# Sixteen small products on TensorE: spread among 32 large ones, or in one burst behind them

## The chip, the cores and the metric

The kernel runs on one core of a Trainium2 chip. The metric is the device time of one execution, in microseconds; lower is better.

## The reference

Two graph layers over N = 8192 nodes with 128 features, each with a residual and a layer norm. The adjacency matrix is 8192 x 8192, 32-bit integers of 0 and 1.

```python
# layer 0: attention
Wh = h @ W
e = (Wh @ a1)[:, None] + (Wh @ a2)[None, :]
e = where(e > 0, e, 0.2 * e)
e = where(adj > 0, e, -9e15)
x = layernorm(x + elu(softmax(e, axis=1) @ Wh))
# layer 1: mean over the neighbours
x1 = a @ x / sum(a, axis=1)
x = layernorm(x + concat([x1, x]) @ weight + bias)
```

## The kernel before

**The first layer.** The exponential of a leaky ReLU of s_i + t_j is one of two products, depending on the sign of s_i + t_j. So the kernel never computes a score for the matmul: it makes two 0/1 masks for each tile (an edge with a positive score, an edge with a negative one) and multiplies them with two sets of factors. The nodes are taken in 32 groups of 256 rows (two tiles of 128). For a group there are four accumulators (two tiles, positive and negative), `acc`, each a sum over 64 column tiles.

The 64 column tiles of a group are done in 8 steps `h` of 8 tiles. One step, `multiply` (lines 653 to 677), is 4 accumulators x 8 tiles = 32 masked products (line 668): a 128x128 mask of one byte per element as the weights, and 259 columns of factors that stream past it. ScalarE makes the sign masks ("levels", line 465) in a ring of 8 slots, VectorE joins them with the edges (lines 974 and 981) in place, and TensorE waits for `mask_ok` ahead of each step. The last masked product of a step signals `mask_used`, for which ScalarE waits before it fills that slot again for the next group. The last product of each accumulator in step 7 signals VectorE, which scales and adds the accumulators (`add_negative`, lines 1010 to 1020: `acc_done` for the first three, `mask_used` for the fourth) before TensorE may start the next group's sum in the same bank.

**The packing.** The edges come as 32-bit integers and are packed into 16-bit words, one bit an edge, which both layers unpack. 512 rows by 2048 columns are a chunk; four chunks make a block of two groups. GpSimd starts the load of a chunk (`load_adj`, line 360, which narrows it to bytes), VectorE shifts and ors its four row tiles into one byte tile (`join`, lines 913 and 916), and TensorE multiplies the byte tile with powers of two (`pack_tile`, line 615): 16 products, each with 128x128 bytes as the weights and 32 columns of `pack_w` that stream past, into a bank of `pack_ps` that alternates with the chunk. The last of them signals `packed`. ScalarE then copies the words out (`copy_words`, line 421), and GpSimd starts the next load into that chunk's slot.

The first four chunks are packed ahead of or between the first steps, without a join: `pack_bits` (line 627) makes 64 products in one row, 4 for each of the 16 positions. All later chunks are packed inside the steps of groups 1 to 29. The order is written out by hand (lines 698 to 705): the dictionary gives for a pair of steps `c` the chunk that is packed in its second step.

```python
group(1, {1: (1, 0), 2: (1, 1), 3: (1, 2)})
group(2, {1: (1, 3), 2: (2, 0), 3: (2, 1)})
group(3, {1: (2, 2), 3: (2, 3)})
with pe.Fori(2, NR - 1) as n:
    group(PAIR * n, {1: (n + 1, 0), 3: (n + 1, 1)})
    group(PAIR * n + 1, {1: (n + 1, 2), 3: (n + 1, 3)})
```

NR is 16. `packable` (line 608), ahead of such a step, waits until the chunk is joined and the words of the chunk before the last are copied out.

**The second layer** (line 746 above all) starts when the first is done, and works from the packed words.

Of the kernel before, what the change touches and what calls it, by code (L numbers as in the profile page):

```python
# [41 lines left out]
UNIT = 16  # L42
HALF = 8
# [15 lines left out]
def adj_resnorm_kernel(nc, x, adj, w0, a0, w1, b1, consts, out):  # L59
# [21 lines left out]
    with ctx:  # L81
# [494 lines left out]
        def _(pe):  # L576
# [35 lines left out]
            def pack_tile(c, j):  # L612

                nibbles = adj_ring[:, c, 0, j * P:(j + 1) * P].bitcast(F8)
                return pe.matmul(pack_ps[c % 2][:, j * WPR:(j + 1) * WPR], nibbles, pack_w[:, 0, :], start=True, stop=True)  # L615
# [37 lines left out]
            def multiply(g, h, factors_in=False, first=False, pack_chunk=None):  # L653

                pe.wait_ge(mask_ok, 8 * g + h + 1)
                pe.sem_inc(masks_there, 1)
                for a in range(2 * TPG):
                    b, neg = a // 2, a % 2
                    if factors_in and a < 2:
                        pe.wait_ge((e_low_ok, f_low_ok)[neg], min(h // 2, UPG - 1) + h // 7 + 1)  # L660
                    if h == 0 and not first:
                        pe.wait_ge(neg_added if neg else pos_scaled, TPG * (g - 1) + b + 1)
                        pe.sem_inc(sums_read, 1)
                    for j in range(HALF):
                        jj = h * HALF + j
                        mask = level_bytes[:, h % MASK_SLOTS, j, b * P:(b + 1) * P] if neg else \
                            edge_bytes[:, (h // 2) % EDGE_SLOTS, (h % 2) * HALF + j, b * P:(b + 1) * P]
                        m = pe.matmul(acc[a][:, 0:WIDE_ROW], mask, factors[:, neg, jj, 0:WIDE_ROW],  # L668
                                      start=(jj == 0), stop=(jj == NJ - 1))
                        if h == 7 and a < 2 * TPG - 1 and j == HALF - 1:  # L670
                            m.then_inc(acc_done, 1)
                        if a == 2 * TPG - 1 and j == HALF - 1:
                            m.then_inc(mask_used, 1)
                        if pack_chunk is not None and j % 2:
                            w = pack_tile(pack_chunk, (a * HALF + j) // 2)
                if pack_chunk is not None:
                    w.then_inc(packed, 1)

            def group(g, packs):
                for c in range(UPG):  # L680
                    for h in (2 * c, 2 * c + 1):
                        n, pack_chunk = packs.get(c, (0, None)) if h % 2 else (0, None)
                        if pack_chunk is not None:
                            packable(n, pack_chunk)
                        multiply(g, h, pack_chunk=pack_chunk)
# [7 lines left out]
            for c in range(UPG):  # L693
                if c == 1:
                    pack_bits(3)
                for h in (2 * c, 2 * c + 1):
                    multiply(0, h, c == UPG - 1 or h % 2 == 0, True)
# [615 lines left out]
```

## Time and profile before

| | us |
|---|---|
| median of 3 runs | 1489.55 (1487.83 to 1490.34) |
| the profiled execution | 1488.95 |
| its span, first to last instruction | 1487.2 |
| TensorE busy in the span | 1449.8 (97%) |
| VectorE busy | 995.0 (67%) |
| ScalarE busy | 936.7 (63%) |

The span holds three parts: some 50 us until the first masked product, the first layer up to about 1000 us, and the second layer. PE stands for TensorE's matmuls, PEld for its weight loads, DVE for VectorE, ACT for ScalarE, POOL for GpSimd. A matmul's end is modelled and runs past the start of the next one, so the pace of a stream of matmuls is read from start to start.

### The profile page before, as it was taken

How to read it: one execution, taken by the hardware profiler on the slowest of the kernel's cores; microseconds unless marked ns; L12 is line 12 of the kernel's file. 1: busy time of each engine (PE TensorE's matmuls, PEld its weight loads, DVE VectorE, ACT ScalarE, POOL GpSimd, SP SyncE). 2: the span in 40 equal slices, each digit the busy share in tenths (PEclk: the TensorE clock that was granted, in tenths of full speed). 3: DMA queues.
4: the chain of work that ended last, by engine and by line, in shares of the span. 5: the costliest groups of instructions: out<-in, count | busy, mean ns of one | idle time of the engine just before them, and what ended most of it. 6: DMA issues, size and time to landing. Idle time of an engine off the chain costs nothing.

```text
span 1487.2 us, 33752 instructions
## 1 busy us (share of the span) xinstructions
PE 1449.8 (97%) x11982; PEld 1095.5 (74%) x11982; DVE 995.0 (67%) x2835; ACT 936.7 (63%) x2289; POOL 118.2 (8%) x199
## 2 busy tenths in 40 slices
PE   7599999999999999999999999999999999999997
PEld 7478888888888888888888888884454545454543
DVE  4997887888788888878878888773433343334332
ACT  6989999999999999999999999940000000000000
POOL 1001100100010010001001000000000000000000
PEclk9789999999999999999999999999999999999999
DMA  9969997788688868877886882041000000000000
GB/s 172 111 75 103 120 102 91 83 94 95 84 87 96 93 78 95 94 88 84 94 95 83 88 96 37 19 116 49 22 19 17 14 21 15 20 14 21 14 14 14
DMA packets 99182, 101.42 MB, mean 68 GB/s; under 512 B 4416, under 2 KB 66368, under 8 KB 99136
## 3 DMA queue, kind: packets, MB, share of 16 engines
q0 software_dynamic: 33792, 67.11, 45.4%
q1 hardware_dynamic: 65344, 33.70, 8.7%
q8 instruction: 28, 0.46, 0.1%
q14 instruction: 18, 0.15, 0.0%
HBM read 289.48 MB, written 12.65 MB: 203 GB/s over the span
## 4 chain that ended last, share of the span: by engine, by line
PE 92%; DVE 1%; DMA 0%; issue 0%; POOL 0%; ACT 0%; SPq 0%; DVEq 0%; POOLq 0%; ACTq 0%
PE acc L668 60%; PE pack_ps L746 29%; PE pack_ps L615 1%; PE turn_ps L768 1%; PE acc L781 1%; PE turn_ps L757 0%; DMA level_ring<-x_rows 0%; POOL one L380 0%; DMA x_parts<-parts 0%; DVE stats L1078 0%; DVE edge_ring L981 0%; DVE level_ring L1177 0%; DVE adj_space L913 0%; DVE mv L1085 0%; DVE level_ring L1090 0%
## 5 line engine op out<-in xcount | busy, mean ns | idle before, releaser
L465 ACT ACTIVATE level_ring<-s_row,cols 128x256 fp8e4<-128x256 f32 x1984 | 803.7, 495 | 0.0
L668 PE MATMUL acc<-factors,edge_ring 128*128 128x259 f16 x4096 | 549.3, 274 | 8.0 <-DVE edge_ring L981 5.6
L668 PE MATMUL acc<-factors,level_ring 128*128 128x259 f16 x4096 | 548.1, 274 | 0.0
L746 PE MATMUL pack_ps<-adj_space,factors 128*128 128x512 fp8e4 x2048 | 449.9, 379 | 0.8 <-issue 0.8
L668 PEld LDWEIGHTS acc<-factors,edge_ring 128*128 128x128 fp8e4 x4096 | 366.1, 98 | 58.0 <-issue 8.6
L668 PEld LDWEIGHTS acc<-factors,level_ring 128*128 128x128 fp8e4 x4096 | 366.5, 98 | 48.9
L746 PEld LDWEIGHTS pack_ps<-adj_space,factors 128*128 128x128 f16 x2048 | 200.4, 98 | 231.9 <-issue 1.1
L974 DVE TENSOR_TENSOR level_ring<-level_ring,edge_ring 128x1024 uint16<-128x1024 uint16 x256 | 171.1, 689 | 104.3 <-ACT level_ring L465 93.9
L1148 DVE TENSOR_SCALAR adj_space<-words 128x512 uint16 (+1 forms) x448 | 96.2, 287 | 146.8 <-PE pack_ps L746 146.7
L615 PE MATMUL pack_ps<-pack_w,adj_space 128*128 128x32 bf16 x960 | 170.7, 178 | 0.0
L981 DVE TENSOR_TENSOR edge_ring<-edge_ring,level_ring 128x1024 uint16<-128x1024 uint16 x256 | 166.7, 683 | 0.1
L564 ACT ACTIVATE level_ring<-pack_ps 128x256 f32<-128x256 f32 x32 | 10.5, 381 | 226.9 <-PE pack_ps L746 226.9
L556 ACT ACTIVATE level_ring<-turn_ps 128x512 f32<-128x512 f32 x16 | 9.6, 597 | 224.1 <-PE turn_ps L757 224.1
L904 DVE TENSOR_SCALAR edge_ring<-words 128x512 uint16 (+1 forms) x448 | 106.4, 298 | 9.1 <-issue 6.6
L378 POOL TENSOR_SCALAR one<-mv 128x2 f32<-128x2 f32 x64 | 18.7, 292 | 1085.1 <-DVE mv L1085 1085.1
L615 PEld LDWEIGHTS pack_ps<-pack_w,adj_space 128*128 128x128 fp8e4 x960 | 91.6, 95 | 14.1
L1177 DVE SCALAR_TENSOR_TENSOR level_ring<-acc,cols,level_ring 128x128 f32<-128x128 f32 x64 | 19.4, 345 | 92.6 <-PE acc L781 92.6
L913 DVE SCALAR_TENSOR_TENSOR adj_space<-adj_space 128x1024 int32<-128x1024 int32 x60 | 73.1, 1219 | 0.0
L360 POOL DMA_DIRECT2D adj_space<-in_adj x64 | 51.3, 802 | 255.9 <-PE pack_ps L615 199.1
L421 ACT ACTIVATE words<-pack_ps 128x512 f32 (+1 forms) x64 | 38.2, 596 | 41.4 <-PE pack_ps L615 41.3
L380 POOL TENSOR_TENSOR one<-one 128x2 f32<-128x2 f32 x64 | 47.9, 749 | 9.5
L1090 DVE TENSOR_SCALAR level_ring<-level_ring,mv,one 128x128 f32<-128x128 f32 x64 | 19.3, 343 | 41.4 <-POOL one L380 41.4
(102 smaller groups left out, 672.4 us busy)
## 6 DMA issues: line engine op xcount, KB each, us to landing
adj_space<-in_adj POOLq DMA_DIRECT2D x64, 1024.0 KB, 14.4
factors<-in_x SPq DMA_DIRECT2D x8, 512.0 KB, 7.1
rows_x<-in_x SPq DMA_DIRECT2D x32, 128.0 KB, 2.1
x_rows<-rows_y SPq DMA_DIRECT2D x32, 128.0 KB, 9.8
x_parts<-parts SPq DMA_DIRECT2D x32, 128.0 KB, 4.4
factors<-x_parts SPq DMA_DIRECT2D x8, 512.0 KB, 4.9
level_ring<-x_rows SPq DMA_DIRECT2D x16, 256.0 KB, 2.8
out<-level_ring SPq DMA_DIRECT2D x32, 128.0 KB, 1.8
```

The source lines that it names most:

```text
L360: pool.dma_start(adj_ring[:, c, :, :], adj_tiles[n, :, :, c * COLS:(c + 1) * COLS]).then_inc(adj_in[c], 16)
L380: pool.tensor_tensor(rstd, var_eps, minus_half, ALU.pow).then_inc(rstd_sem, TPG)
L421: act.activation(row_words[:, n, c * WPU:(c + 1) * WPU], pack_ps[c % 2][:, 0:WPU], ACT.Copy)\
L465: a = act.activation(level_bytes[:, h % MASK_SLOTS, j, :], s_row[:, slot, :], ACT.Relu, bias=t_big[:, h * HALF + j:h * HALF + j + 1], scal ...
L615: return pe.matmul(pack_ps[c % 2][:, j * WPR:(j + 1) * WPR], nibbles, pack_w[:, 0, :], start=True, stop=True)
L668: m = pe.matmul(acc[a][:, 0:WIDE_ROW], mask, factors[:, neg, jj, 0:WIDE_ROW], start=(jj == 0), stop=(jj == NJ - 1))
L746: m = pe.matmul(pack_ps[slot][:, :], factors[:, 0, jj, part * F:(part + 1) * F], ring_1_bytes[:, c, j, :], start=(jj == 0 and part == 0), ...
L904: d = dve.tensor_scalar(to, src, 6 - k, EDGES, ALU.logical_shift_left, ALU.bitwise_and)
L913: dve.scalar_tensor_tensor(out=pair[:, 0], in0=pair[:, 1], scalar=1, in1=pair[:, 0], op0=ALU.logical_shift_left, op1=ALU.bitwise_or).then_ ...
L974: dve.tensor_tensor(level, level, edge_ring[:, c % EDGE_SLOTS, k * HALF:(k + 1) * HALF, :], ALU.bitwise_and).then_inc(neg_ready, 1)
L981: dve.tensor_tensor(edges, edges, level_ring[:, (2 * c + k) % MASK_SLOTS, :, :], ALU.bitwise_xor)\
L1148: d = dve.tensor_scalar(to, src, 6 - k, EDGES, ALU.logical_shift_left, ALU.bitwise_and)
```

## The change

In a step that packs, the 16 packing products are no longer placed behind every second masked product. They follow in one row behind the 32nd masked product of the step, and the last of them still signals `packed`. The signal `mask_used` stays on the 32nd masked product, which now has none of the packing products ahead of it.

```diff
                         if a == 2 * TPG - 1 and j == HALF - 1:
                             m.then_inc(mask_used, 1)
-                        if pack_chunk is not None and j % 2:
-                            w = pack_tile(pack_chunk, (a * HALF + j) // 2)
                 if pack_chunk is not None:
+                    for j in range(UNIT):
+                        w = pack_tile(pack_chunk, j)
                     w.then_inc(packed, 1)
```

## Rows read from the trace of the kernel before

**Rows 1.** The page: busy time and share, then the granted clock in 40 slices.
```profile
PE 1449.8 (97%) x11982; PEld 1095.5 (74%) x11982; DVE 995.0 (67%) x2835; ACT 936.7 (63%) x2289; POOL 118.2 (8%) x199
...
PEclk9789999999999999999999999999999999999999
```

**Rows 2.** The page: the chain that ended last, by line.
```profile
PE acc L668 60%; PE pack_ps L746 29%; PE pack_ps L615 1%; PE turn_ps L768 1%; PE acc L781 1%; PE turn_ps L757 0%; DMA level_ring<-x_rows 0%; POOL one L380 0%; DMA x_parts<-parts 0%; DVE stats L1078 0%; DVE edge_ring L981 0%; DVE level_ring L1177 0%; DVE adj_space L913 0%; DVE mv L1085 0%; DVE level_ring L1090 0%
```

**Rows 3.** TensorE's waits at line 668: us in total, times, longest.
```profile
PE acc L668 <- DVE edge_ring L981: 5.6, 2, 5.1
...
PE acc L668 <- DVE part_sums L1011: 2.4, 1, 2.4
```

**Rows 4.** Busy time by stretches (two bursts, a slow stretch, all packing steps).
```profile
core 0: us, PE busy (x) PEld busy (x) DVE busy (x) ACT busy (x) POOL busy (x), PEclk, DMA share, GB/s
...
49.50:51.00 1.50, 1.50 (x60) 1.50 (x60) 1.50 (x2) 1.50 (x6) 0.00 (x0) 0.50 1.04 111
59.40:60.90 1.50, 1.50 (x62) 1.50 (x63) 1.47 (x4) 1.50 (x5) 0.00 (x0) 1.00 1.08 116
...
93.00:97.00 4.00, 3.53 (x19) 2.54 (x20) 3.76 (x13) 4.00 (x11) 0.00 (x0) 0.57 1.06 108
...
105.00:942.00 837.00, 837.00 (x8296) 738.33 (x8294) 680.26 (x1744) 787.76 (x1948) 78.15 (x114) 1.00 0.78 88
```

**Rows 5.** Timeline of TensorE, plain steps and one that packs: start, us, what.
```profile
402.18 1.05 PE L668 MATMUL acc<-factors,edge_ring 128*128 128x259 f16 x8
...
412.82 0.39 PE L668 MATMUL acc<-factors,edge_ring 128*128 128x259 f16 x2
413.04 0.18 PE L615 MATMUL pack_ps<-pack_w,adj_space 128*128 128x32 bf16 x1
413.07 0.38 PE L668 MATMUL acc<-factors,edge_ring 128*128 128x259 f16 x2
...
416.75 0.18 PE L615 MATMUL pack_ps<-pack_w,adj_space 128*128 128x32 bf16 x1
416.77 1.05 PE L668 MATMUL acc<-factors,edge_ring 128*128 128x259 f16 x8
```

**Rows 6.** Timeline of TensorE: the first packing step, and behind the last.
```profile
105.62 0.39 PE L668 MATMUL acc<-factors,edge_ring 128*128 128x259 f16 x2
...
942.01 1.05 PE L668 MATMUL acc<-factors,edge_ring 128*128 128x259 f16 x8
...
997.87 1.05 PE L668 MATMUL acc<-factors,level_ring 128*128 128x259 f16 x8
```

**Rows 7.** Timeline of TensorE: two bursts of the first chunks.
```profile
49.39 1.89 PE L627 MATMUL pack_ps<-pack_w,adj_space 128*128 128x32 bf16 x64 [7.77 <-DMA adj_space<-in_adj]
...
59.35 1.76 PE L627 MATMUL pack_ps<-pack_w,adj_space 128*128 128x32 bf16 x64 [0.44 <-DMA adj_space<-in_adj]
```

**Rows 8.** Waits of all engines: us in total, times, longest.
```profile
POOL adj_space L360 <- PE pack_ps L615: 199.1, 27, 13.8
...
ACT words L421 <- PE pack_ps L615: 41.3, 60, 1.3
DVE cols L1018 <- PE acc L668: 30.0, 60, 0.6
```

**Rows 9.** Timeline of VectorE over the end of a group.
```profile
417.14 0.16 DVE L1018 TENSOR_TENSOR cols<-acc,one 128x1 f32 x1 [0.57 <-PE acc L668]
417.28 0.48 DVE L1020 SCALAR_TENSOR_TENSOR row_sums<-acc,cols,part_sums 128x258 f32<-128x258 f32 x1
...
419.91 1.28 DVE L981 TENSOR_TENSOR edge_ring<-edge_ring,level_ring 128x1024 uint16<-128x1024 uint16 x2
```

**Rows 10.** Packing weight loads: all of line 615 (mean ns), then one burst's timeline.
```profile
L615 PEld LDWEIGHTS pack_ps<-pack_w,adj_space 128*128 128x128 fp8e4 x960 | 91.6, 95 | 14.1
...
59.34 1.66 PEld L627 LDWEIGHTS pack_ps<-pack_w,adj_space 128*128 128x128 fp8e4 x64 [0.72 <-DMA adj_space<-in_adj]
```

**Rows 11.** Timeline of TensorE behind its longest wait in masked products.
```profile
75.62 1.94 PE L668 MATMUL acc<-factors,level_ring 128*128 128x259 f16 x8
77.35 1.94 PE L668 MATMUL acc<-factors,edge_ring 128*128 128x259 f16 x8
```

## The prediction

> **What bounds the kernel now.** I read the page first. TensorE (PE) is busy for 97% of the span, and its granted clock is at 9 tenths or more in all but two of 40 slices [rows 1]. The chain that ended last says where: 60% of the span lies on the masked products of line 668, 29% on the products of the second layer (line 746), and only 1% on the packing products of line 615 that the change moves [rows 2]. The whole stake is therefore small before anything is worked out.
>
> A busy TensorE can still be waiting in small pieces, so the waits come next. In the masked products it waited three times, 8.0 us in all [rows 3]. The table by stretches places these waits: from 105 us to 942 us, which holds every step with packing products, TensorE is busy for 837.00 of 837.00 us at a granted clock of 1.00 [rows 4]. In that stretch the time is set by how fast TensorE takes its own stream of products; nothing that another engine gets earlier can shorten it.
>
> **What a packing product costs where it stands now.** The timeline of TensorE has both kinds of step. A plain run of masked products goes from 402.18 to 412.82 us, twelve groups of eight: 10.64 / 96 = 110.8 ns each. A step with packing products goes from 412.82 to 416.77, 3.95 us for 32 masked products and 16 packing ones [rows 5]. The end of a product is modelled (0.18 us for a packing product), so I count from start to start. For more digits I use the long stretch: the first step that packs begins at 105.62, the first step after the last one at 942.01, and the plain products behind it take (997.87 - 942.01) / 63 = 0.8867 us per eight, 3.547 us per step [rows 6]. By the loops, the stretch holds 29 groups of 8 steps less the first 3, so 229 steps, of which 60 pack (three in group 1, three in group 2, two in group 3, and 13 rounds of four) and 169 don't. 836.39 - 169 x 3.547 = 236.95 us, over 60 is 3.949 us. A packing step thus costs 0.402 us more than a plain one, and one packing product 0.402 / 16 = 25.1 to 25.2 ns. That already includes any delay that it causes to the masked product behind it, which starts 0.03 us after it [rows 5].
>
> **What it costs in a burst.** The kernel has such bursts: the first four chunks are packed by 64 products in a row, with the same operands (128x128 weights of one byte, 32 columns) and a new weight load for each. The one at 59.35 us takes 1.76 us; less the modelled end, (1.76 - 0.18) / 63 = 25.1 ns from start to start, at a granted clock of 1.00. The one at 49.39 takes (1.89 - 0.18) / 63 = 27.1 ns, at half the clock [rows 4, 7]. The stretch of the change has the full clock, so I take 25.1 ns and keep 27.1 as the upper end.
>
> **The sum.** Removed: 16 packing products between masked ones, at 25.1 to 25.2 ns. Added: the same 16 behind the step's 32nd masked product, at 25.1 ns. The masked product that used to follow each packing product follows a masked one instead, at 110.8 ns as in a plain step. So the step goes from 3.949 us to 3.547 + 16 x 0.0251 = 3.949 us: nothing, with a reading error of about 0.3 ns x 960 = 0.3 us either way. At the upper price it is 2.0 ns x 960 = +1.9 us. No weight load, transfer or wait is added or removed. The wait for the chunk to be packable still stands ahead of the step's first masked product.
>
> **What else moves.** Two signals leave TensorE at other times. The one that a chunk is packed stays at the end of the step, within 0.02 us. ScalarE's copy of the words, which waits 41.3 us in 60 times for it, and GpSimd's next adjacency load behind it, keep their times [rows 8]. The one that a step's masks are used stood 0.40 us later than it will, since 16 packing products were mixed in; ScalarE's next scores and VectorE's sums of the last accumulator may start up to 0.40 us sooner. VectorE waited 30.0 us in 60 times for TensorE at line 1018, a wait of 0.5 us on average that shrinks in the steps that end a group. It gives TensorE nothing: the sums of the fourth accumulator end at 417.76, and the next group, which began at 416.77, wants that accumulator only after three groups of eight, at 419.43. The masks of the next group's third step start their last pass at 419.91 and both halves are there at 421.19, while TensorE gets to them at 416.77 + 2 x 3.55 = 423.87 [rows 5, 9]. That margin of 2.7 us is the cover, and the change adds to it. No queue of SyncE or GpSimd is passed by anything moved.
>
> **Rival 1, slower: the weight loads come into the open.** Between masked products, the load of a packing product's weights can run while a product of 259 columns streams; in a burst it has only products of 32 columns to hide behind. One such load lasts 95 ns [rows 10]. If a burst went at that pace, a step would cost 16 x 0.095 = 1.52 us in place of 0.40, 60 steps +67 us: 1556 us. From 28.3 ns per product on (3.0 us / 960 above 25.2) it would show as slower. Against it: in the burst at 59.35, the 64 loads take 1.66 us together [rows 10], 26 ns each, so loads of 95 ns overlap one another. The Trainium skill has a rule that speaks for this rival ("TensorE: Matmul & The Clock Gate", section "LDWEIGHTS (loading the stationary operand)"): a load lasts its columns over 1.2 GHz, by which 128 columns are 107 ns, and a burst paying that in full would add about 79 us by estimate. The duration in the trace is near that figure, but the spacing of the 64 loads doesn't bear out that it has to be paid. I give this rival 0.03.
>
> **Rival 2, slower: the clock falls.** A burst works the array less densely than masked products do. If the granted clock halved for one plain step behind each burst, eight masked products would take 77.35 - 75.62 = 1.73 us instead of 0.887, as they did after a long wait [rows 11]; 4 x 0.84 x 60 is +202 us, and one such step costs 3.4 us, enough to show. Against it: the burst of 64 at 59.35, four times as long and with idle time around it, held 1.00, and the half clock came where TensorE had waited (0.57 from 93 to 97 us) [rows 3, 4]. 0.01.
>
> **Rival 3, faster: a burst costs less than the mix.** By columns alone, a product of 32 would take 32 / 259 x 110.8 = 13.7 ns; 11.4 ns x 960 would save 11 us: 1478.5 us. Against it stands the same burst, which never went below 25 ns on average. That earlier mask signals pay is the other way to get faster, and the 837.00 busy us leave no wait to be paid from. 0.03.
>
> **How the numbers follow.** The profiled execution has 1488.95 us around its span of 1487.2, and the runs shown have a median of 1489.55, 0.6 above. The change adds 0.0 us to either, and I forecast 1489.4, between the two and near the median. The likeliest case, no change, has 0.92. The range takes the upper price (+1.9 us gives 1491.3) and the scatter of the three runs (1487.83 to 1490.34): 1487.4 to 1491.3. About 0.2%, 3 us, is what a measurement of this kernel can tell from no change. Faster has 0.03 (rival 3), slower 0.05: rivals 1 and 2, and 0.01 for a cost that no row here has.
>
> **What would show it.** In the changed kernel's timeline, a packing step should still last 3.95 us: four groups of eight masked products without a break, 0.887 us apart, then one row of 16 packing products of 0.55 us (15 x 0.025 + 0.18), the next step 0.40 us after the burst's start. TensorE should be busy throughout from 105 to 942 us at 1.00, and the step after the last that packs should start at 942 us. VectorE's wait at line 1018 should shrink, ScalarE's at line 421 should not. I am wrong if the packing products of a burst stand more than 28 ns apart, if a gap opens before the first or behind the last of them, or if the clock in that stretch is below 1.00.

## The result, and the profile after

The changed kernel takes 1492.88 us (median of 20 runs, 1490.73 to 1493.94), the kernel before 1488.04 us (20 runs, 1487.45 to 1490.34). The ratio is 1.0025, 95% interval 1.0019 to 1.0031: slower by some 3.7 us. I had forecast 1489.4 us and no change. The times of both kernels fall into two clusters some 2.2 us apart, before at 1487.5 to 1488.6 and 1489.6 to 1490.3, after at 1490.7 to 1491.4 and 1492.4 to 1493.9; median against median, the change costs 3.1 us in the lower and 3.2 us in the upper.

Both profiled executions can be cut at the same two places, the first packing step and the first step behind the last one. This is TensorE's timeline of the changed kernel at these places, beside [rows 6]:

```profile
107.45 0.72 PE L668 MATMUL acc<-factors,edge_ring 128*128 128x259 f16 x5
...
946.89 1.05 PE L668 MATMUL acc<-factors,edge_ring 128*128 128x259 f16 x8
```

| us | before | after | difference |
|---|---|---|---|
| ahead of the first packing step | 105.62 | 107.45 | +1.83 |
| packing steps and those between them | 836.39 | 839.44 | +3.05 |
| behind them | 545.2 | 545.2 | 0.0 |

The 1.83 us lie where neither kernel packs inside a step. In the 14 kernels profiled here that first part took 103.9 to 107.5 us, with bursts and without (103.92 in a kernel with mixed steps, 104.37 in one with bursts), so I read it as scatter of the start. What the change costs is the 3.05 us in the middle, which agrees with the 3.1 to 3.2 us between like clusters.

There, the table by stretches (columns as in [rows 4]) has TensorE no longer busy throughout, still at a granted clock of 1.00:

```profile
107.45:946.89 839.44, 838.05 (x8290) 741.81 (x8288) 682.66 (x1744) 787.38 (x1948) 76.56 (x114) 1.00 0.78 88
```

Busy time counts only gaps past the modelled end of a product, so I look at the bursts themselves. The timeline of TensorE in the middle of a group, then at the end of group 5:

```profile
404.39 0.55 PE L615 MATMUL pack_ps<-pack_w,adj_space 128*128 128x32 bf16 x16
404.79 1.05 PE L668 MATMUL acc<-factors,edge_ring 128*128 128x259 f16 x8
```

```profile
243.11 0.55 PE L615 MATMUL pack_ps<-pack_w,adj_space 128*128 128x32 bf16 x16
243.80 1.05 PE L668 MATMUL acc<-factors,edge_ring 128*128 128x259 f16 x8
```

The first is what I forecast: the burst lasts 0.55 us with the modelled end, and the next step starts 0.40 us after it began. The second has the same burst, but the next step starts 0.69 us after its start. Of the 60 bursts, 48 are like the first, with at most 0.06 us behind the last packing product, and 12 like the second: 0.26 to 0.32 us. The 12 are the ends of the odd groups from 5 to 27. The even groups end with the same burst and the same waits, and have no gap. What the odd ones have besides is the end of the loop's body: `with pe.Fori(2, NR - 1) as n` (line 701) holds two groups, and TensorE's sequencer jumps back 12 times. (The sequencer is the part of an engine whose register work, waits and branches the profile lists apart from the products.)

The instructions of that line (name, count, min/median/max ns, first and last start in us) are the sequencer's own (PEldq):

```profile
...
L701 PEldq ALU_OP  x13: 32/32/32, 242.9 to 946.3; - x13
L701 PEldq COMPARE_BRANCH  x13: 76/208/249, 243.0 to 946.4; - x13
```

The first jump begins at 242.9, ahead of the burst's first product at 243.11: the sequencer is ahead of the array. From the branch at 243.0 to the next group's first product it takes 0.79 us; the burst is through after 0.51. The first weight load behind the burst says the same, and names no engine that was waited for:

```profile
243.77 0.79 PEld L668 LDWEIGHTS acc<-factors,edge_ring 128*128 128x128 fp8e4 x8 [0.20 <-issue]
```

In the kernel before, the branch of that jump starts at 240.3, and the next group's first product at 241.69, 1.36 us later, right behind the last product of the mixed step. The branch in its rows of line 701, then TensorE's timeline:

```profile
L701 PEldq COMPARE_BRANCH  x13: 76/208/249, 240.3 to 940.6; - x13
```

```profile
241.67 0.18 PE L615 MATMUL pack_ps<-pack_w,adj_space 128*128 128x32 bf16 x1
241.69 0.49 PE L668 MATMUL acc<-factors,edge_ring 128*128 128x259 f16 x3
```

The jump was there; it was hidden.

### The profile page after: what moved, and what is told of

Same layout as the page of the kernel before. It is cut to its first block, busy times and chain, and to the rows that moved or that the text cites. A ratio compares the mean times of both kernels' runs of the same rounds, so it can differ in the third digit from the quotient of the medians.

```text
span 1492.1 us, 33752 instructions
## 1 busy us (share of the span) xinstructions
PE 1450.9 (97%) x11982; PEld 1099.5 (74%) x11982; DVE 998.2 (67%) x2835; ACT 936.6 (63%) x2289; POOL 116.6 (8%) x199
## 4 chain that ended last, share of the span: by engine, by line
PE 93%; DVE 1%; issue 0%; POOL 0%; ACT 0%; DVEq 0%; POOLq 0%; ACTq 0%
PE acc L668 59%; PE pack_ps L746 30%; PE pack_ps L615 2%; PE turn_ps L768 1%; PE acc L781 1%; PE turn_ps L757 0%; POOL one L380 0%; DVE edge_ring L981 0%; DVE level_ring L1177 0%; DVE adj_space L913 0%; DVE stats L1078 0%; DVE level_ring L1090 0%; DVE level_ring L974 0%; DVE edge_ring L904 0%; DVE mv L1085 0%
## 5 line engine op out<-in xcount | busy, mean ns | idle before, releaser
L668 PE MATMUL acc<-factors,edge_ring 128*128 128x259 f16 x4096 | 539.9, 275 | 11.0 <-DVE edge_ring L981 7.2
L668 PE MATMUL acc<-factors,level_ring 128*128 128x259 f16 x4096 | 539.0, 274 | 0.0
L668 PEld LDWEIGHTS acc<-factors,edge_ring 128*128 128x128 fp8e4 x4096 | 396.7, 98 | 65.7 <-issue 12.7
L668 PEld LDWEIGHTS acc<-factors,level_ring 128*128 128x128 fp8e4 x4096 | 401.6, 98 | 54.1
L421 ACT ACTIVATE words<-pack_ps 128x512 f32 (+1 forms) x64 | 38.1, 596 | 44.6 <-PE pack_ps L615 44.6
L916 DVE SCALAR_TENSOR_TENSOR adj_space<-adj_space 128x512 int32<-128x512 int32 x60 | 41.5, 692 | 2.0
L615 PEld LDWEIGHTS pack_ps<-pack_w,adj_space 128*128 128x128 fp8e4 x960 | 32.8, 96 | 1.6
```

The costliest lines, as they stand in the source:

```text
L916: dve.scalar_tensor_tensor(out=joined[:, c, 0, :], in0=joined[:, c, TPG, :], scalar=TPG, in1=joined[:, c, 0, :], op0=ALU.logical_shift_lef ...
```

## The experiments

Theory J: the jump is late behind a burst. By it, the sequencer can be ahead of the array by a fixed number of products only; 16 packing products of 0.025 us are then less time than the jump takes, and mixed with masked products of 0.11 us they were more. Rival S: a burst costs more than the mix wherever it stands, by 0.05 us each. Rival V: VectorE's sums of the accumulators are late at the end of a group.

The stretch is that of the table above, from the first product of the first packing step (in e3, a packing product) to the first step behind the last; the gap is from start to start, in a full stream 0.03 behind a packing product and 0.11 behind a masked one. Ratios are against the runs of the kernel before on the same chips.

| kernel | stretch, us | gaps of jumps, us | median, us | ratio |
|---|---|---|---|---|
| before | 836.39 | none | 1488.04 | |
| after | 839.44 | 12 of 0.26 to 0.32 | 1492.88 | 1.0025 (1.0019 to 1.0031) |
| e1 mixed at loop end | 836.28 | none | 1489.39 | 0.9996 (0.9987 to 1.0005) |
| e2 burst at loop end only | 839.34 | 12 of 0.26 to 0.31 | 1493.55 | 1.0026 (1.0014 to 1.0037) |
| e3 burst in front | 836.19 | none | 1489.64 | 1.0002 (0.9993 to 1.0011) |
| e4 half the jumps | 882.80 | 5 of 5.97 to 6.18 | 1534.12 | 1.0299 (1.0285 to 1.0313) |
| e9 six rounds out | 837.85 | 6 of 0.27 to 0.37 | 1491.14 | 1.0018 (1.0008 to 1.0027) |
| e10 no loop | 836.19 | none | 1487.81 | 0.9997 (0.9987 to 1.0006) |
| e5 two behind | 839.32 | 12 of 0.35 to 0.40 | 1493.03 | 1.0028 (1.0018 to 1.0038) |
| e6 four behind | 837.38 | 12 of 0.18 to 0.24 | 1491.00 | 1.0006 (0.9996 to 1.0015) |
| e12 eight behind | 836.19 | none | 1488.74 | 1.0001 (0.9991 to 1.0011) |
| e7 burst, longer jump | 847.18 | 12 of 0.87 to 0.91 | 1500.83 | 1.0082 (1.0065 to 1.0099) |
| e8 mixed, longer jump | 836.73 | 12 of 0.03 to 0.08 | 1487.88 | 0.9997 (0.9987 to 1.0006) |
| e11 mixed, longer still | 843.99 | 12 of 0.62 to 0.69 | 1495.65 | 1.0047 (1.0030 to 1.0063) |

**Which burst costs.** Two kernels split the 60 steps into the 13 that end the loop's body (12 of which are followed by a jump; `loop_end` is true there) and the other 47. The diff is shortened here: the lines that pass `loop_end` down are left out, and conditions are written more simply.

```diff
...
-                        if pack_chunk is not None and j % 2:
+                        if pack_chunk is not None and loop_end and j % 2:       # e2: not loop_end
                             w = pack_tile(pack_chunk, (a * HALF + j) // 2)
                 if pack_chunk is not None:
+                    if not loop_end:                                            # e2: loop_end
+                        for j in range(UNIT):
+                            w = pack_tile(pack_chunk, j)
...
```

> The last packing step of the loop's body is mixed as before; the other 47 packing steps keep the burst behind the masked products. Theory J (TensorE's sequencer jumps back to the loop's head behind a burst that is too short to cover the jump): no product waits at a group's end; from the first packing step to the first step behind the last, 836.4 us as in the kernel before (839.4 with all bursts), time within 0.1% of before. Rival V (VectorE's sums are late at a group's end): the even groups never waited, so as J here. Rival S (a burst costs more than the mix wherever it stands): 47 of 60 bursts remain, +2.4 us.

> Only the last packing step of the loop's body (13 of 60) has its 16 packing products in a burst; the others are mixed as before. J: the 12 jumps back cost what they cost with all bursts, 0.24 to 0.29 us each, +3.1 us in all, the stretch of packing steps 839.5 us. S: 13 of 60 bursts, +0.7 us.

With 47 bursts left, e1 has no gap and the time of before. With 13 bursts, e2 has the whole loss. S falls: it wanted +2.4 us of e1 and +0.7 us of e2.

**The burst at the other end of the step.** In e3 the same 16 products stand ahead of the step's masked products.

```diff
                 pe.wait_ge(mask_ok, 8 * g + h + 1)
                 pe.sem_inc(masks_there, 1)
+                if pack_chunk is not None:
+                    for j in range(UNIT):
+                        w = pack_tile(pack_chunk, j)
+                    w.then_inc(packed, 1)
                 for a in range(2 * TPG):
...
-                if pack_chunk is not None:
-                    for j in range(UNIT):
-                        w = pack_tile(pack_chunk, j)
-                    w.then_inc(packed, 1)
```

> The burst of 16 stands ahead of the step's 32 masked products, in all 60 packing steps. J: masked products are queued ahead of every jump, so no gap; the stretch of packing steps 836.1 to 836.4 us, time within 0.1% of before. S: the burst costs the same wherever it stands, +3 us. V: the group ends with masked products, as in the kernel before, and VectorE has the 0.4 us less that it had there, so as J.

No gap. From the first packing product at 104.11 to 940.29 the stretch is 836.19 us, the same as in e10 and e12, and the time is that of before.

**The number of jumps.** The order of products and waits stays that of the changed kernel; only the loop is cut differently. e4 puts two rounds into the body and takes one out, e9 takes six rounds out, e10 all 13.

```diff
+            def block(n):                                # e4, with the two lines of the body
...
+            block(2)
+            with pe.Fori(0, (NR - 4) // 2) as m:
+                block(2 * m + 3)
+                block(2 * m + 4)
```

```diff
+            for n in range(2, 8):                        # e9; e10: range(2, 15), and no Fori
+                group(PAIR * n, {1: (n + 1, 0), 3: (n + 1, 1)})
+                group(PAIR * n + 1, {1: (n + 1, 2), 3: (n + 1, 3)})
-            with pe.Fori(2, NR - 1) as n:
+            with pe.Fori(8, NR - 1) as n:
```

> All 60 bursts stand behind the masked products; TensorE's loop holds two rounds in its body and one round is taken out of it, so it jumps back 5 times in place of 12. J: five gaps of 0.24 to 0.29 us, +1.3 us, the stretch of packing steps 837.5 us. S and V: the order of products and waits is that of the changed kernel, so its time, +3 us, 839.4 us.

> All 60 bursts stand behind the masked products; six of the loop's 13 rounds are written out ahead of it, so TensorE jumps back 6 times in place of 12, and the loop's body keeps its size. J: six gaps of 0.24 to 0.31 us, all in groups 17 to 27, +1.6 us. S and V: +3 us.

> All 60 bursts stand behind the masked products; all 13 rounds are written out, and TensorE has no loop in this part. J: no gap behind any burst, the stretch of packing steps 836.1 to 836.4 us, time within 0.1% of before, unless fetching a longer program costs something of its own. S and V: +3 us.

e9 and e10 answer: six jumps cost 837.85 - 836.19 = 1.66 us of stretch, no jump costs nothing, with all 60 bursts in place. V falls here, as S does. In e10, the end of group 5 that showed the gap above is closed:

```profile
242.34 0.56 PE L615 MATMUL pack_ps<-pack_w,adj_space 128*128 128x32 bf16 x16
242.74 1.05 PE L668 MATMUL acc<-factors,edge_ring 128*128 128x259 f16 x8
```

e4 missed by far, +44 us where I expected 1.3. Its five jumps are its five large gaps, so the loss begins where J puts it, but one costs 6 us, not 0.3. The five make 30 of the 46 us that its stretch is longer than before; the rest lies behind them, in products at a slower pace and a second, shorter wait. Timeline of TensorE at the first of them, then the table by stretches for what follows, then the instruction queue's line in the list of DMA queues:

```profile
356.63 0.56 PE L615 MATMUL pack_ps<-pack_w,adj_space 128*128 128x32 bf16 x16
363.02 1.89 PE L668 MATMUL acc<-factors,edge_ring 128*128 128x259 f16 x8 [5.83 <-issue]
```

```profile
363.00:366.00 3.00, 2.98 (x14) 2.07 (x15) 1.48 (x6) 3.00 (x9) 0.00 (x0) 0.50 1.06 111
```

```profile
q8 instruction: 97, 1.59, 0.4%
```

The changed kernel's line of that queue:

```profile
q8 instruction: 28, 0.46, 0.1%
```

And that of e10, which has no loop:

```profile
q8 instruction: 83, 1.36, 0.3%
```

The queue that brings instructions moved 1.13 MB more in e4. The body of two rounds has 2 x 576 products with a weight load each, 2304 instructions; that of one round has 1152. The Trainium skill bears on this ("Runtime: NRT & Kernel Launch", section "Instruction fetch mechanics"): TensorE's instruction memory has room for 2048 instructions and is filled ahead in a straight line, and a taken branch whose target isn't in the window that it holds has to fetch it before execution goes on. The traffic of e4 agrees with that. More traffic alone costs nothing here: e10 moved 0.90 MB more than the changed kernel, in a straight line, and lost no time. That the 6 us are the fetch is argued from this traffic; no run varied the size of the body further. The clock stood at half behind each jump (0.50 above), which added to the loss. e4 thus measures another price of a jump, and e9 took its place.

**How much has to stand behind the burst.** In e5, e6 and e12, the burst stands ahead of the last 2, 4 and 8 masked products of its step, instead of behind the step.

```diff
+                        if pack_chunk is not None and a == 2 * TPG - 1 and j == HALF - 2:   # e6: 4, e12: 8
+                            for i in range(UNIT):
+                                w = pack_tile(pack_chunk, i)
+                            w.then_inc(packed, 1)
                         m = pe.matmul(acc[a][:, 0:WIDE_ROW], mask, factors[:, neg, jj, 0:WIDE_ROW],
...
-                if pack_chunk is not None:
-                    for j in range(UNIT):
-                        w = pack_tile(pack_chunk, j)
-                    w.then_inc(packed, 1)
```

> All 60 bursts stand ahead of the last two masked products of their step. J with a queue that holds a fixed number of products: the same number is queued at the jump, two of them masked, which give 2 x 85 ns more cover; the gap at the 12 jumps falls from 0.24 to 0.29 us to about 0.1 us, +1.2 us in all. If the cover doesn't depend on what is queued: gaps of 0.24 to 0.29 us remain, +3 us.

> All 60 bursts stand ahead of the last four masked products of their step. J, with the cover that the last 18 products ahead of the jump give: 4 x 0.11 + 14 x 0.025 = 0.79 us in place of 0.62, so the jump lacks 0.07 to 0.12 us in place of 0.24 to 0.28; 12 start-to-start gaps of 0.18 to 0.23 us behind a masked product (0.11 in a full stream), +1.1 us in all. If what is queued doesn't matter: gaps of 0.35 us as with two behind.

> All 60 bursts stand ahead of the last eight masked products of their step. J: the last 18 products are 8 x 0.11 + 10 x 0.025 = 1.14 us, more than the 0.87 that the jump needs; no gap, time within 0.1% of before. If what is queued doesn't matter: 12 gaps of 0.35 us, +3 us.

e5 went against my number: the gaps lack 0.24 to 0.29 us, as without the two products. The count in the trace shows why. From the jump's first instruction to the loop's head, 17 products start, in the kernel before, the changed one, e3, e5, e6 and e12 alike; the jump begins 0.02 us after the product ahead of these 17 starts. So 18 products cover it. From the first of them to the loop's head, the uncovered jumps of the changed kernel, e5 and e6 take 0.86 to 0.92 us. In the changed kernel the 18 are two masked and 16 packing ones, in e5 16 packing and two masked ones: 2 x 0.11 + 16 x 0.025 = 0.62 us both times. I had overlooked the two masked products ahead of the burst. With four behind, the 18 are four masked and 14 packing, 0.79 us, and e6 was forecast by that rule: gaps of 0.18 to 0.23, measured 0.18 to 0.24. The timeline of e6 at the end of group 5:

```profile
242.58 0.60 PE L672 MATMUL acc<-factors,level_ring 128*128 128x259 f16 x4
243.14 1.05 PE L672 MATMUL acc<-factors,edge_ring 128*128 128x259 f16 x8
```

Four masked products take 0.44 us and the next step starts 0.56 us after the first of them. In time alone e6 can't be told from before; the gaps decide. With eight behind (e12), the 18 last 1.14 us and the gap is gone.

**The length of the jump.** e7 (on the changed kernel) and e8 (on the kernel before) make it longer by four increments of a semaphore for which no one waits; e11 is e8 with eight.

```diff
                 group(PAIR * n + 1, {1: (n + 1, 2), 3: (n + 1, 3)})
+                for _ in range(4):                       # e11: 8
+                    pe.sem_inc(sums_read, 1)
```

> The changed kernel with four more semaphore increments in TensorE's program at the loop's end, which no one waits for, about 0.15 us of the sequencer each. J: the jump is already uncovered, so all of it shows: gaps of 0.8 to 0.9 us, 12 x 0.6 = +7 us on the changed kernel. V or S: hidden, nothing on the changed kernel.

> The kernel before with the same four more semaphore increments at the loop's end that cost the changed kernel 0.6 us a jump. J: its jump has 0.57 to 0.62 us to spare; gaps of at most 0.05 us, at most +0.6 us in all. If an increment costs TensorE's products its time wherever it stands: +7 us.

> The kernel before with eight more semaphore increments at the loop's end. J: the spare 0.6 us are used up by the first four, the other four show: gaps of 0.55 to 0.65 us behind the last packing product, +7 us. If a jump between mixed products is always hidden: nothing.

The same four increments cost the changed kernel 847.18 - 839.44 = 7.7 us (0.5 of it behind the loop's last round, where there is no jump) and the kernel before 836.73 - 836.39 = 0.3 us. Four more, on the kernel before, cost 7.3 us. TensorE's timeline at the first jump, of e7:

```profile
242.45 0.55 PE L615 MATMUL pack_ps<-pack_w,adj_space 128*128 128x32 bf16 x16
243.74 1.05 PE L668 MATMUL acc<-factors,edge_ring 128*128 128x259 f16 x8 [0.74 <-issue]
```

and of e8:

```profile
239.98 0.18 PE L615 MATMUL pack_ps<-pack_w,adj_space 128*128 128x32 bf16 x1
240.06 1.05 PE L668 MATMUL acc<-factors,edge_ring 128*128 128x259 f16 x8
```

So the mixed step had some 0.6 us to spare over the jump and the burst lacks (839.44 - 836.19) / 12 = 0.27 us. No version beat the kernel before: e3, e10 and e12 keep all 60 bursts, remove the loss and come out within 0.1% of it.

## Why the prediction was wrong

- The stake was small and TensorE sets the time of this stretch: right. All of the loss in it is TensorE's own time, its sequencer's.
- The price of a packing product, 25.1 to 25.2 ns in the mix and in a burst: right. In the changed kernel's bursts they stand 25 ns apart, and without the jumps the stretch is 836.19 us (e10) against 836.39.
- Rivals 1 to 3: none happened. The weight loads of a burst overlap as they did in [rows 10], the granted clock is 1.00, and a burst is no cheaper than its 25 ns.
- The signals to other engines: right. VectorE's wait at line 1018 shrank from 30.0 us in 60 [rows 8] to 21.0 in 48, and gave TensorE nothing. ScalarE's copies waited 44.6 us in 60 times, 41.3 before. From the waits of all engines, after:

```profile
DVE cols L1018 <- PE acc L668: 21.0, 48, 0.5
```

- The step that failed is in the sum: "No weight load, transfer or wait is added or removed." No instruction was added, but a wait was: I priced the end of a packing step at the 0.03 us that the mixed steps show, for all 60, and did not ask what hid the sequencer's work at that place. Behind 12 of the 60 stands the loop's jump, 0.75 to 0.80 us from branch to product, which stood nowhere in the sum, and its cover was the very thing that the change moved: the 18 products in the queue shrank from about 1.5 us to 0.62. Beyond the 0.025 us of a full stream the 12 gaps add up to 3.20 us, of the 3.25 us by which the stretch is longer than without jumps (e10).
- The range followed from that: its upper end was 27 ns per product in all bursts, and a rival with a price for the loop's end was not among the cases. "A cost that no row here has" got 0.01.
- Of the signs that I named for being wrong, the gap behind a burst is the one that came, and TensorE was not busy throughout (838.05 of 839.44 us).

## What to carry to other kernels

When work moves on an engine, ask what its sequencer does behind it: here a jump with its register work and waits was hidden by the products that were queued ahead, and there were 17 of them whatever time they took. Short products cover little, so the last ones ahead of a loop's jump should be long; eight masked products behind the burst (e12), or the burst in front of the step (e3), bring the whole loss back. The profile before shows the cover, 1.36 us: the start of the branch in the rows of the loop's line, beside the start of the first product behind it. What the jump itself takes, 0.75 to 0.80 us, only the uncovered jumps of the later kernels show.

## What the runs showed of the hardware

- TensorE's sequencer was 17 products, each with its weight load, ahead at a jump, whether they lasted 0.60 us from the jump's first instruction (burst), 1.46 (mix) or 1.97 (masked products alone, e3).
- A jump back with the waits at the loop's head took 0.75 to 0.80 us from branch to the next product where it was not hidden (0.85 at the first jump of e9), of which the branch itself 0.21 to 0.25. A semaphore increment ahead of it added some 0.15 us (e7).
- A loop's body of 2304 products and weight loads made every jump back cost 6 us and half the clock behind it (e4), where 1152 cost 0.3 us even in the uncovered case.
